# Other memory layouts, with fewer and longer transfers, for five intermediates of a delta-rule attention kernel

## What is computed

```python
def step(carry, xs):
    W_t, W_avg = carry
    i, Ki, Qi, Vi, Bi = xs
    KiT = jnp.swapaxes(Ki, -1, -2)
    T = jnp.tril(Bi @ KiT, k=-1)
    inv = jnp.linalg.inv(eyeC + T)
    Ui = inv @ (Vi - Bi @ W_t)
    W_new = W_t + KiT @ Ui
    ...
    O_i = Qi @ W_avg * a + Qi @ W_t * c + T_mat * (Qi @ KiT) @ Ui
    return ((W_new, W_avg_new), O_i)
```

## Time and profile before

| | us |
|---|---|
| three runs | 1509.09, 1510.67, 1511.9 |
| median | 1510.67 |
| the profiled execution | 1518.6 |
| its span in the trace | 1516.8 |

### The profile page before, as it was taken

One profiled execution on the slowest core, in us unless ns is written; L12 is line 12 of the kernel. 1 busy time (PEld: TensorE's weight loads), 2 busy tenths in 40 slices (PEclk: granted clock), 3 DMA queues, 4 the chain that ended last, 5 costly groups with the idle time before them and its releaser, 6 DMA issues. The chain is left out here.

```text
span 1516.8 us, 28805 instructions
## 1 busy us (share of the span) xinstructions
PE 1179.7 (78%) x10846; PEld 791.1 (52%) x10846; DVE 764.9 (50%) x1707; ACT 515.8 (34%) x1049; POOL 388.6 (26%) x366
## 2 busy tenths in 40 slices
PE   4766456566656561688697987999999999999997
PEld 2543334353535351466475764555666666666664
DVE  4599849586868683567646873221111212121211
ACT  3454245353636360433243332331122222222221
POOL 6100113131202021513226003662022222222222
PEclk9788679777878785867888997999999999999999
DMA  7644566868585968777687747953122323232322
GB/s 269 188 101 134 120 178 142 251 140 248 128 255 121 259 136 235 199 224 224 179 246 225 230 152 278 377 171 103 32 40 46 48 45 49 44 49 43 49 44 31
DMA packets 237366, 228.68 MB, mean 151 GB/s; under 512 B 88980, under 2 KB 177972, under 8 KB 236080
## 3 DMA queue, kind: packets, MB, share of 16 engines
q1 hardware_dynamic: 202944, 194.28, 45.3%
q0 software_dynamic: 16368, 19.96, 7.5%
q10 hardware_dynamic: 17920, 12.59, 2.8%
HBM read 117.39 MB, written 115.62 MB: 154 GB/s over the span
## 5 line engine op out<-in xcount | busy, mean ns | idle before, releaser
L1644 DVE TENSOR_TENSOR hid_all<-p_s,silu 128x512 f32<-128x512 f32 x103 | 71.3, 692 | 378.8 <-PE p_s L1495 249.7
L1694 POOL DMA_INDIRECT out_h<-y_sb,x_in x71 | 110.6, 1558 | 360.9 <-DVE y_sb L1656 343.0
L1552 ACT ACTIVATE silu<-p_m 128x512 f32<-128x512 f32 x103 | 61.5, 597 | 328.0 <-PE p_m L1488 223.4
L804 DVE SCALAR_TENSOR_TENSOR cv<-raw,conv_sb,cv 128x512 f32<-128x512 f32 x144 | 117.5, 820 | 83.6 <-ACT raw L698 81.7
L175 DVE TENSOR_TENSOR xt<-xt,prod 128x62 f32<-128x62 f32 (+15 forms) x248 | 142.0, 572 | 4.3
L172 DVE TENSOR_TENSOR prod<-nx,xt 128x62 f32<-128x62 f32 (+15 forms) x248 | 138.4, 558 | 2.5
L1510 PE MATMUL p_y<-wo,hid_all 128*128 x568 | 134.4, 379 | 0.8 <-ACT hid_all L1569 0.8
L1488 PE MATMUL p_m<-wi,xT_c 128*128 x284 | 133.5, 592 | 0.5 <-ACT xT_c L1565 0.5
L1495 PE MATMUL p_s<-ws,xT_c 128*128 x284 | 133.6, 593 | 0.0
L288 PE MATMUL p_item<-xbd,bv_i 128*32 128x128 f32 x1024 | 46.8, 340 | 108.4 <-issue 39.5
L575 PE MATMUL p_p<-xT,wqkv_sb 128*128 128x512 f32 x192 | 108.6, 705 | 0.7 <-issue 0.7
(11 more groups left out here) (155 smaller groups left out, 2093.9 us busy)
## 6 DMA issues: line engine op xcount, KB each, us to landing
slots_in_dram<-xt SPq DMA_DIRECT2D x18, 520.0 KB
x_in<-slots_in_dram SPq DMA_DIRECT2D x71, 130.0 KB, 2.1
q_channels_dram<-qT SPq DMA_DIRECT2D x128, 64.0 KB
k_tokens_dram<-h SPq DMA_DIRECT2D x32, 256.0 KB
chunk_gram_dram<-h SPq DMA_DIRECT2D x32, 256.0 KB
beta_kv_dram<-h SPq DMA_DIRECT2D x8, 1024.0 KB
nx<-chunk_gram_dram SPq DMA_DIRECT2D x8, 1024.0 KB, 6.3
scores_dram<-h SPq DMA_DIRECT2D x8, 1024.0 KB
```

Source lines behind the costliest of these rows:

```text
L804: ins = dve.scalar_tensor_tensor(cv[:, p, m, :], raw[:, p, m, j:j + L], conv_sb[:, p, m, j:j + 1], cv[:, p, m, :], ALU.mult, ALU.add)
L1644: dve.tensor_tensor(dst, p_s[n % 2][:], silu[n % 2][:], ALU.mult).then_inc(S["hid_ready"], 1)
L1694: pool.indirect_dma_start(token_rows, bass.IndirectOffsetOnAxis(x_in[s % X_IN][:, D:D + 1].bitcast(U32), 0), y_sb[s % 2][:], None, compute ...
```

## The change

Five intermediates get another place in device memory.

- The inverse lies as `xt` holds it, by head pair, chunk and row: the store is one transfer (128 rows of 8 KB) instead of eight made of 256 B pieces. The four `xbd` loads of an item now gather 256 B pieces, 32x8x64 elements each, where they read rows of 2 KB.
- q lies by head quad, channel and token: eight stores instead of 16, 4x16x512 elements each, with 2 KB pieces; the `q_i` load reads 512 B pieces.
- k lies by batch and token: one store instead of four. In stage B `kk_b` reads four batches of 32 rows; before, these 128 rows followed each other.
- y and the queries share one buffer `yq_out`, one tensor `yq_dram`, one store an item and one load `yq` a step (128 rows of 4 KB). The store stands where the queries' store stood, so y is now stored an item later, and ACT, before it writes y, waits for that store of two items ago.
- `zo` lies by batch and token: one store an item instead of four; the `zo` load of a step reads four batches of 32 rows.

`load_step` now waits for the u sum and the o sum of step s - 2 before its first load. Nothing else changes its order. SP issues 65 transfers for a batch with items, where it issued 99. The core of the diff:

```diff
-    x_dram = nc.dram_tensor("chunk_inverse_dram", [B, L, H * C], F32, kind="Internal").ap()
+    x_dram = nc.dram_tensor("chunk_inverse_dram", [B, HP, NC_BATCH, C, ROW], F32, kind="Internal").ap()
...
-    qT_dram = nc.dram_tensor("q_channels_dram", [B, TILES, P, HQ, P], F32, kind="Internal").ap()
-    kk_dram = nc.dram_tensor("k_tokens_dram", [NC_BATCH, B, C, 2 * D], F32, kind="Internal").ap()
-    y_dram = nc.dram_tensor("y_channels_dram", [B // GROUP, NC_BATCH, P, GROUP, HQ * C], F32, kind="Internal").ap()
-    qy_dram = nc.dram_tensor("queries_dram", [B // GROUP, NC_BATCH, P, GROUP, HQ * C], F32, kind="Internal").ap()
-    zo_dram = nc.dram_tensor("z_and_inner_dram", [NC_BATCH, B, C, 2 * D], F32, kind="Internal").ap()
+    qT_dram = nc.dram_tensor("q_channels_dram", [B, HQ, P, L], F32, kind="Internal").ap()
+    kk_dram = nc.dram_tensor("k_tokens_dram", [B, L, 2 * D], F32, kind="Internal").ap()
+    yq_dram = nc.dram_tensor("y_and_queries_dram", [B // GROUP, NC_BATCH, P, GROUP, 2 * HQ * C], F32, kind="Internal").ap()
+    zo_dram = nc.dram_tensor("z_and_inner_dram", [B, L, 2 * D], F32, kind="Internal").ap()
...
-            for g in range(HP):
-                sp.dma_start(x_dram[b, :, g * ROW:(g + 1) * ROW].rearrange("(c k) x -> c k x", k=C),
-                             xt[b % 2][g * NC_BATCH:(g + 1) * NC_BATCH].rearrange("p k e i -> p k (e i)")
-                             ).then_inc(s_xst, 16)
-
-        STORES = 16 * (16 + CH + 2)
+            sp.dma_start(x_dram[b].rearrange("g c k x -> (g c) (k x)"),
+                         xt[b % 2][:].rearrange("p k e i -> p (k e i)")).then_inc(s_xst, 16)
+
+        STORES = 16 * (8 + 1 + 2)
...
-            sp.wait_ge(s_xst, 16 * HP * (b + 1))
+            sp.wait_ge(s_xst, 16 * (b + 1))
             sp.wait_ge(s_st, STORES * (b + 1))
             for c in range(CH):
-                sp.dma_start(xbd[tok(c), c].rearrange("p h i -> p (h i)"), x_dram[b, t * P + c * C:t * P + (c + 1) * C]
+                sp.dma_start(xbd[tok(c), c].rearrange("p h i -> p (h i)"), x_dram[b, :, t * CH + c].rearrange("g k x -> k g x")
...
-            sp.dma_start(q_i[:], qT_dram[b, t]).then_inc(s_q_in, 16)
-
-        def store_y(sp, r):
-            b, t, i = r // TILES, r % TILES, r % 2
-            sp.wait_ge(T["y_ready"], r + 1)
-            sp.dma_start(y_dram[b // GROUP, t * CH:(t + 1) * CH, :, b % GROUP].rearrange("c p x -> p c x"),
-                         y_out[i][:].rearrange("p c n i -> p c (n i)")).then_inc(s_y_st[i], 16)
-
-        def store_rest(sp, r):
+            sp.dma_start(q_i[:], qT_dram[b, :, :, t * P:(t + 1) * P].rearrange("n p l -> p n l")).then_inc(s_q_in, 16)
+
+        def store_item(sp, r):
             b, t, i = r // TILES, r % TILES, r % 2
             sp.wait_ge(T["z_ready"], r + 1)
             sp.wait_ge(T["inner_ready"], r + 1)
-            for c in range(CH):
-                sp.dma_start(zo_dram[t * CH + c, b], zo_out[i][tok(c)].rearrange("p w h d -> p (w h d)")
-                             ).then_inc(s_zo_st[i], 16)
+            sp.dma_start(zo_dram[b, t * P:(t + 1) * P], zo_out[i][:].rearrange("p w h d -> p (w h d)")).then_inc(s_zo_st[i], 16)
+            sp.wait_ge(T["y_ready"], r + 1)
             sp.wait_ge(T["q_ready"], r + 1)
-            sp.dma_start(qy_dram[b // GROUP, t * CH:(t + 1) * CH, :, b % GROUP].rearrange("c p x -> p c x"),
-                         qy_out[i][:].rearrange("p c n i -> p c (n i)")).then_inc(s_qy_st[i], 16)
+            sp.dma_start(yq_dram[b // GROUP, t * CH:(t + 1) * CH, :, b % GROUP].rearrange("c p x -> p c x"),
+                         yq_out[i][:].rearrange("p c w n i -> p c (w n i)")).then_inc(s_yq_st[i], 16)
...
-            store_y(sp, r)
             if r:
-                store_rest(sp, r - 1)
+                store_item(sp, r - 1)
...
-                act.wait_ge(s_y_st[r % 2], 16 * (r // 2))
-            act.activation(y_out[r % 2][:].rearrange("p c n i -> p n c i"), bank[:].rearrange("p (n c i) -> p n c i", n=HQ, c=CH),
+                act.wait_ge(s_yq_st[r % 2], 16 * (r // 2))
+            act.activation(yq_out[r % 2][:, :, 0].rearrange("p c n i -> p n c i"), bank[:].rearrange("p (n c i) -> p n c i", n=HQ, c=CH),
...
-                        for f in range(4):
-                            for m in range(2):
-                                for w in range(2):
-                                    sp.dma_start(qT_dram[b, :, f * C + w * DH:f * C + (w + 1) * DH, m::2].rearrange("t d n l -> d n t l"),
-                                                 qT[m * 4 * DH + f * DH:m * 4 * DH + (f + 1) * DH].rearrange("d n (t l) -> d n t l", t=TILES)
-                                                 ).then_inc(s_st, 16)
+                        for n in range(HQ):
+                            for w in range(2):
+                                sp.dma_start(qT_dram[b, n].rearrange("(f w d) l -> w f d l", w=2, d=DH)[w],
+                                             qT[n % 2 * 4 * DH:(n % 2 + 1) * 4 * DH, n // 2]).then_inc(s_st, 16)
                         sp.wait_ge(s_kt, b * 2 + 2)
                         sp.wait_ge(s_ktri, b * TILES + TILES)
-                        for c in range(CH):
-                            sp.dma_start(kk_dram[:, b].rearrange("(t c) i x -> c i t x", c=CH)[c],
-                                         kk[tok(c)].rearrange("p t h w d -> p t (h w d)")).then_inc(s_st, 16)
+                        sp.dma_start(kk_dram[b].rearrange("(t p) x -> p t x", p=P),
+                                     kk[:].rearrange("p t h w d -> p t (h w d)")).then_inc(s_st, 16)
...
+                        if c % CH == 0:
+                            sp.wait_ge(s_zo_st[t % 2], 16 * done)
+                            sp.wait_ge(s_yq_st[t % 2], 16 * done)
                         if s >= 2:
                             sp.wait_ge(S["u_summed"], s - 1)
-                        if c % CH == 0:
-                            sp.wait_ge(s_y_st[t % 2], 16 * done)
-                            sp.wait_ge(s_zo_st[t % 2], 16 * CH * done)
-                            sp.wait_ge(s_qy_st[t % 2], 16 * done)
+                            sp.wait_ge(S["o_summed"], s - 1)
                         if c:
-                            sp.dma_start(yy[i][:].rearrange("p b n i -> p (b n i)"), y_dram[g, c].rearrange("p b x -> p (b x)")
-                                         ).then_inc(s_yy[i], 16)
-                        if s >= 2:
-                            sp.wait_ge(S["o_summed"], s - 1)
-                        sp.dma_start(zo[i][:].rearrange("p w d -> p (w d)"),
-                                     zo_dram[c, b:b + GROUP].rearrange("b i x -> (b i) x")).then_inc(s_zo[i], 16)
+                            sp.dma_start(yq[i][:].rearrange("p b w n i -> p (b w n i)"), yq_dram[g, c].rearrange("p b x -> p (b x)")
+                                         ).then_inc(s_yq[i], 16)
+                        sp.dma_start(zo[i][:].rearrange("p w d -> p (w d)"), zo_dram[b:b + GROUP, c * C:(c + 1) * C]
+                                     ).then_inc(s_zo[i], 16)
                         if chunk(s) < NC_BATCH - 1:
                             if s >= 2:
                                 sp.wait_ge(S["w_summed"], states(s - 2))
                             sp.dma_start(kk[i][:].rearrange("p n x -> p (n x)"),
-                                         kk_dram[c, b:b + GROUP].rearrange("b i x -> (b i) x")).then_inc(s_kk[i], 16)
-                        if c:
-                            sp.dma_start(qq[i][:].rearrange("p b n i -> p (b n i)"), qy_dram[g, c].rearrange("p b x -> p (b x)")
-                                         ).then_inc(s_qq[i], 16)
+                                         kk_dram[b:b + GROUP, c * C:(c + 1) * C]).then_inc(s_kk[i], 16)
```

More of the change, by code:

```diff
@@ L196, in build @@
         yz_ch = sb(tail, "yz_ch", [P, HQ, P])
-        y_out = [sb(tail, f"y_out{i}", [P, CH, HQ, C]) for i in range(2)]
+        yq_out = [sb(tail, f"yq_out{i}", [P, CH, 2, HQ, C]) for i in range(2)]
         yz_tok = sb(tail, "yz_tok", [P, H, 2 * DH])
@@ L201, in build @@
         sy_out = [sb(tail, f"sy_out{i}", [P, CH, HQ, C]) for i in range(2)]
-        qy_out = [sb(tail, f"qy_out{i}", [P, CH, HQ, C]) for i in range(2)]
         s_st = tail.enter_context(nc.semaphore("kv_stored"))
@@ L206, in build @@
         s_s_in = tail.enter_context(nc.semaphore("item_scores_loaded"))
-        s_bv_in, s_y_st, s_zo_st, s_qy_st = ([tail.enter_context(nc.semaphore(f"{n}{i}")) for i in range(2)]
-                                                     for n in ("item_bv_loaded", "y_stored", "zo_stored", "queries_stored"))
+        s_bv_in, s_zo_st, s_yq_st = ([tail.enter_context(nc.semaphore(f"{n}{i}")) for i in range(2)]
+                                                     for n in ("item_bv_loaded", "zo_stored", "y_queries_stored"))
         T = {n: tail.enter_context(nc.semaphore("item_" + n)) for n in (
@@ L275, in sum_queries @@
             pool.wait_ge(T["sy_ready"], r + 1)
[L276 removed]
```

(4 more changed lines are left out.)

26 lines of the change are left out of this document (12 added, 14 removed).

## The result

The changed kernel took 1533.3 us (median, 1531.86 to 1538.14) where the kernel before took 1509.92: 1.0159 times as long, 95% interval 1.0132 to 1.0185. Forecast were 1543 us and a range of 1488 to 1563, so the sign and the likeliest case held; of the +32 us forecast, 1533.3 - 1509.92 = 23.4 came.

A forecast was written before the change was run, and what follows sets the result against it. The prediction took PE's expert stage from 917 us, untouched, as the chain, so only stages A and B count: -11.7 (A) + 1 (q stores) + 43 (B) = +32 us, carried to the median: 1543 us, range 1488 to 1563.

The forecast's parts named there:

- the likeliest case: Whole kernel: zo and kk_b loads and q stores run on four DMA engines; +32 us, chance 0.75, own range 1526 to 1563.
- The plain step: End of stage B, 834.7 to 898.9 us: steps of 5.81 us become 7.9 us, limited by the four busiest engines.
- Stage B's sum: 600 to 900 us, 32 steps: window surcharges from loads of zo and kk_b on four engines, together +43 us.
- the surcharge in the item steps: Stage B's steps with items: 3.9 us more on the busiest engines per step loaded; +13.5 from 760 to 809 us.
- Stage A's sum: Up to 597 us, eight batches: earlier Gram stores less slower xbd loads, -11.7 us, with 1 us added for q stores.
- DVE's one long gap: Stage A, 10.93 us idle in batch 4, repeated in 5 to 7: the whole -11.7 us would come out of it.
- the second Gram store then waits for DVE: Stage A, batch 4: SP would reach this store before DVE's tile at 349.2, so it goes 2.6 us sooner.
- The short reads: xbd loads now read 256 B pieces at 23 ns each: +0.8 us at each load on the path.
- Rival 3: xbd loads: 256 B reads cost the gathers' 111 ns, +45 us at eight loads, less 26: 1530 us; chance 0.04.
- The single inverse store: Stage B, twice: eight SP issues (8.43 and 8.83 us) become one of 0.89 us, 7.5 to 7.9 us saved each time.
- rival 1: Stage B: all sixteen engines share the new loads, so it gains 13.6 us; together -26, 1485 us; chance 0.15.
- Rival 2: Stage A: busy DMA engines eat the earlier issue and DVE's gap stays; -13.6 us alone, 1497 us; chance 0.06.

The follow-up runs named there:

- e1: The changed kernel with zo and kk_b each loaded in four transfers, one per batch, instead of one; 1500.64 us, ratio to before 0.9914.
- e2: The kernel before with only zo and k placed by batch and token and loaded as in the changed kernel; 1552.98 us, ratio 1.0241.
- e3: The changed kernel with zo loaded as two transfers of two batches each, kk_b still one transfer; 1604.33 us in one run.
- e4: The changed kernel with the q store as sixteen transfers of 16x2x512 elements instead of eight of 4x16x512; 1534.11 us, ratio 1.0113.
- e8: e1 with kk_b loaded in one transfer again, as in the changed kernel, zo still in four; 1508.35 us, ratio 0.9945.
- e7: e1 with zo stored in four transfers an item instead of one, same place in memory; 1516.29 us, ratio 1.0013.
- e6: e1 with step 12's loads issued right after the last inverse store, ahead of the loads that wait for its landing; 1491.28 us, ratio 0.985.
- e5: e1 with the inverse as before: eight stores of 256 B pieces, xbd read in rows of 2 KB; 1509.07 us, ratio 0.9968.
- e10: e6 with k by chunk in memory again, four stores a batch, kk_b one load of 128 rows; 1494.04 us, ratio 0.9888.

## Why the prediction was right, and where it was not

**Which case.** The loads of `zo` and `kk_b` on four engines: shown by the packet counts, by stretches at a quarter of the engines, by e1, e2 and e3. The rule of the Trainium skill's page "DMA: Bandwidth & Descriptors", section "Why a DMA increments its semaphore by 16 and not by 1", agrees with these runs for four (207723 packets, 100 GB/s) and for two (50 GB/s).

**The plain step.** Forecast 0.68 x 5.81 + 3.9 = 7.9 us, measured 7.96 (7.67 in e2 and e4, whose plain steps load `zo` and `kk_b` in the same form, so a difference of 0.3 us between two such kernels means nothing). That the limit is the sum of work on the busiest engines is supported by this agreement, by the slices of 835 to 907 us, of which only 11 in 320 show fewer than four busy engines, and by e8. PE's share falls with it and so does its clock: granted 0.88 in the window above where it was 1.00, and at the lower of its two levels the same two matmuls take 1.2 us instead of 0.6 to 0.7. The sum had no term for the clock; whether it adds to the step, or hides in the time that PE waits anyway, no run tells.

**Stage B's sum, +43, measured +23.** The term that was mis-sized is the surcharge in the item steps. For steps 0 to 12 I had the four engines eat SP's saving and add 11 us. Measured: 148.7 us, as long as e1 without any four-engine load (148.6). For 12 to 17 I had +13.5, measured 5.1 over e1; for 17 to 31 +18.3, measured 26.0 over e1. Busy shares of the windows before were taken as work that the four engines would have as well. But a packet takes longer when many are under way: the packed traces have 2 KB packets at 96 to 110 ns on average in the windows before, against a median of 84, and at 92 ns in the plain steps after. So the share overstates the work. As an estimate, with every packet of those windows at the median of its size, the work is 35.0, 41.5, 19.6 and 33.4 us instead of 44.8, 47.6, 21.8 and 41.2. With the prediction's own additions the first three windows then stay within their length (53.9 of 56, 63.4 of 68, 32.8 of 33), so the loads hide, and the fourth has 54.7 against 49: +5.7, where 5.1 was measured. That is argued from the traces and not from a run. By the same estimate a plain step would have 0.62 x 5.84 + 3.9 = 7.5 us, under the 7.67 to 7.96 measured: that the overstated share gave 7.9 there is in part luck.

**Stage A's sum, -10.7, measured -11.2** in the profiled run at stage B's first issue. The total is right, but two steps in it are wrong. One is that the whole would come out of DVE's one long gap: the gaps of batches 4, 5 and 6 were 10.93, 10.72 and 9.19 us before and are 10.55, 9.34 and 9.37, 1.6 us less together where 5.4 were forecast. The other is that the second Gram store then waits for DVE. I had worked out 1.9 us less of SP's issues and still took 2.6 us sooner. From beta\*k,v to the Gram stores SP gained 1.5 us, and remains 1.7 us behind DVE. e7 confirms the price instead: three issues, 1.4 us a batch. What made up the difference was batch 3 (-6.2 us by the start of `nx`, 280.69 to 274.49; a second gap of DVE, 4.59 us at 279.57, is gone there) and small gains in the others. Kernels with the same stage A began B at 589.8, 588.7, 584.3 and 589.1 (e1, e3, e6, e8), so that this term itself is known to 5 or 6 us, and its agreement with the forecast is in part luck. And 3.7 us are given back at once: the first `zo` load of stage B takes longer, issued at 588.26 and used at 595.11 (6.9 us) where it had been 599.42 to 602.54 (3.1 us):

```profile
588.26 0.58 SPq L964 DMA_DIRECT2D zo<-z_and_inner_dram  x1
...
595.11 1.19 PE L1020 MATMUL p_u_turn_x<-zo,cst 128*128 128x256 f32 x2 [31.96 <-DMA zo<-z_and_inner_dram]
```

With e1's four transfers it is 592.17 to 595.52, 3.4 us, so it is again the form of the load.

**The short reads.** +0.8 us a load was forecast. From the issue of `nx` to the item that waits for the next `xbd` batches 3 to 6 take 10.80 us on average before, 11.48 after, 11.03 in e1 and 10.80 in e5, where the rows are 2 KB again: +0.2 to 0.7. Rival 3 is out: 256 B reads are as quick as 256 B writes.

**The single inverse store.** SP's part came as forecast (8.43 and 8.83 us, now 0.55 and 0.32), and e5 gives its worth, 7 us in steps 0 to 12. But rival 1 had given it 13.6, and the likeliest case the same before the four engines ate it. After the second one, SP waits for a megabyte to land, 731.16 - 722.43 = 8.7 us, where from first issue to the `xbd` load it had been 749.75 - 737.84 = 11.9. The prediction allowed 1 us for this landing and named a wait of 10 us behind the store as something that would not be there; in e1 the landing took 4.6. PE's wait at step 12 stays (9.39 after 9.67) because the step's own loads are queued behind a wait that doesn't concern them. e6 took that away: 7.6 us in steps 0 to 12, of which 2.4 were lost again by step 17.

**Rival 2** would have shown itself by a gap of batch 4 that is still 10.9 us. It is 10.55, nearly that; yet stage A became 11.2 us shorter in the profiled runs, and no kernel with the same stage A began B later than 589.8, where it had been 597.06. So the gap in that one batch was a poor sign, and rival 2 is out by the time of the stage.

**Rival 1** gave 1485 for sixteen engines everywhere; e1, the nearest kernel, took 1500.6. Of the missing 15.6 us the landing just named is 3.6; the rest is put down to SP's six further issues a step, which e7 showed not to be free in item steps, but no run has sixteen engines without them and the order of the change, so that this stays an inference.

## What to carry to other kernels

In these runs a transfer's outermost entries, on either side, set how many DMA engines it gets (two, four, or sixteen from sixteen entries on); a layout that merges transfers but leaves four (or two) outer entries gives a quarter (or an eighth) of the bandwidth, and loads the same few engines for everyone else. Look for it in the packet count and in slices that stand at 0.25. It costs little while the busiest engines have room in a step (0.26 us a plain step for one load in e8), and all of its time beyond that. More transfers help only if each has enough outer entries of its own: two halves with two entries each were slower than one with four. And behind a store that must land before a load, issue first what doesn't depend on it.

## What had not been expected of the hardware

- The small completion packets count a transfer's engines: 16, 4 or 2 of 4 bytes each, to the packet (207723 against 207726 forecast; e3, with two transfers on two engines in place of one on four, 207725).
- Splitting a transfer in two made it slower (e3, 1604 us), in four much faster (e1, 1501 us, with both loads split). By the shares of e3's trace the two halves ran on the same two engines.
- 256 B pieces read from memory across eight places cost 18 ns in the median, like 256 B pieces written: 14 GB/s for one engine. The prediction had 22 and 23 ns, from a share of a full queue.
- Kernels with the same code in stage A (after, e1, e3, e6, e8) began stage B between 584.3 and 589.8 us, so terms of 2 us need repeated runs, and the three issues that e10 saves could not be told.
